# A transformer layer on one core: the last batch's shared up products moved from the late stage to the output stage

## The reference

```
x = x + cross_attention(layernorm(x), ctx)
xt = layernorm(x).reshape(2048, 512)
ids, probs = top 2 of (xt @ Wr + br + gate_bias), softmax over the two
routed:  u = xt @ Wup[e] + bup[e];  g = silu(u @ Wgate[e] + bgate[e]) * u;  eo = g @ Wdown[e] + bdown[e]
shared:  su = xt @ Wsu + bsu;  sg = silu(su @ Wsg + bsg) * su;  so = sg @ Wsd + bsd
out = x + sum over e of probs[e] * eo[e] + so
```

## Time and profile before

| | us |
|---|---|
| median of 3 runs | 1020.87 |
| lowest and highest run | 1019.53, 1021.21 |
| the profiled execution | 1023.9 |
| its span, first to last instruction | 1022.3 |
| PE busy in it | 927.3 |
| VectorE busy in it | 659.0 |
| GpSimd busy in it | 620.0 |
| ScalarE busy in it | 464.1 |
| output stage | from about 439 to 570.7 |
| routed stage | from 570.7 to 956.0 |
| late stage | from 956.0 to 1022.3 |

### The profile page before, as it was taken

How to read it: one execution, slowest core, us unless ns; L and a number is a source line. 1 busy time by engine, 2 the same in 40 slices (tenths; PEclk the granted TensorE clock), 3 DMA queues, 4 the chain that set the end, 5 groups by cost and what they waited for, 6 DMA issues and landing times. The chain is left out here.

```text
span 1022.3 us, 17154 instructions
## 1 busy us (share of the span) xinstructions
PE 927.3 (91%) x5077; PEld 406.1 (40%) x5078; DVE 659.0 (64%) x1026; ACT 464.1 (45%) x846; POOL 620.0 (61%) x565
## 2 busy tenths in 40 slices
PE   3799885799989999989999599999999999999998
PEld 1354542122212222246644244444544554554443
DVE  7787776688878788357765155554555555444388
ACT  3365565688878787522451022322322322322440
POOL 5465446377777674443047489898999999000373
PEclk9899998699999999989999699999999999999999
DMA  8135436345445432134427655555565664435566
GB/s 277 32 108 145 133 112 176 99 168 174 161 170 183 143 99 65 40 125 135 175 104 278 205 165 175 176 192 163 199 183 170 201 187 162 123 114 188 217 197 234
DMA packets 104521, 162.31 MB, mean 159 GB/s; under 512 B 10904, under 2 KB 53912, under 8 KB 104080
## 3 DMA queue, kind: packets, MB, share of 16 engines
q1 hardware_dynamic: 91520, 116.45, 35.1%
q0 software_dynamic: 12896, 45.10, 13.2%
q10 hardware_dynamic: 48, 0.05, 0.0%
HBM read 108.08 MB, written 53.48 MB: 158 GB/s over the span
## 5 line engine op out<-in xcount | busy, mean ns | idle before, releaser
L1060 DVE TENSOR_REDUCE nm<-quad 128x4 bf16<-128x1984 f32 x62 | 138.3, 2231 | 37.3 <-PE quad L1121 37.3
L1013 ACT ACTIVATE p_t<-a_psT 128x512 f32<-128x512 f32 x256 | 138.9, 595 | 48.0 <-PE a_psT L1136 46.6
L963 POOL TENSOR_TENSOR p_sum<-p_t,p_t 128x512 f32<-128x512 f32 x64 | 81.0, 1274 | 56.0 <-ACT p_t L1013 55.7
L1907 PE MATMUL quad<-w_exp,e_xT 128*128 x456 | 107.4, 387 | 7.3 <-issue 3.4
L1907 PE MATMUL e_psY<-w_exp,e_gT 128*128 x456 | 110.7, 380 | 0.9 <-ACT e_y L1848 0.9
L1907 PE MATMUL quad<-w_exp,e_uT 128*128 x456 | 106.6, 385 | 2.5 <-DVE e_uT L1862 2.5
L1136 PE MATMUL a_psT<-q_stk,k_stk 98*128 98x512 f16 x256 | 84.6, 401 | 12.1 <-ACT p_t L1013 9.4
L210 POOL TENSOR_TENSOR w_exp<-e_raw,w_exp 128x1024 f32 (+1 forms) x42 | 90.1, 2145 | 6.0 <-POOL e_raw L207 4.5
L202 POOL TENSOR_TENSOR w_exp<-e_raw,ws_tile 128x1024 f32 (+1 forms) x42 | 80.2, 1910 | 5.6 <-DMA e_raw<-in_L_ffn_Wup_dram 4.7
L1834 ACT ACTIVATE e_gT<-e_psGT 128x512 f16<-128x512 f32 x38 | 22.7, 597 | 124.7 <-PE e_psGT L1897 124.7
L1889 DVE TENSOR_TENSOR e_g<-e_g,e_u 128x512 f32<-128x512 f32 x38 | 58.6, 1542 | 26.4 <-ACT e_g L1855 26.4
(11 more groups left out here) (333 smaller groups left out, 1859.6 us busy)
## 6 DMA issues: line engine op xcount, KB each, us to landing
xs_dram<-zero SPq DMA_DIRECT2D x38, 256.0 KB, 7.2
e_x<-xs_dram SPq DMA_DIRECT2D x38, 256.0 KB, 4.1
bias<-in_L_ffn_bup_dram SPq DMA_DIRECT2D x38, 256.0 KB, 3.7
bias<-in_L_ffn_bgate_dram SPq DMA_DIRECT2D x38, 256.0 KB, 3.7
ys_dram<-e_y SPq DMA_DIRECT2D x38, 256.0 KB, 3.8
q_dram<-q_st SPq DMA_DIRECT2D x24, 256.0 KB, 3.0
k_dram<-k_st SPq DMA_DIRECT2D x24, 256.0 KB, 3.7
q_stk<-q_dram SPq DMA_DIRECT2D x64, 96.0 KB
```

What stands on the lines that cost most here:

```text
L963: pool.tensor_tensor(p_sum[:, w % SUMS, :], probs(w, 0), probs(w, 1), ALU.add).then_inc(s["sum_1"], 1)
L1013: act.activation(probs(w, k), psT[:, k % 2], ACT.Exp, scale=SCALE / (QS * QS)).then_inc(s["exp"], 1)
L1060: dve.tensor_reduce(nm[:, i, :, 0:1].rearrange("p h o -> p (h o)"), psS[:, :, 0:NMAIN], AX.X, ALU.max, negate=True)
L1907: ins = pe.matmul(dst[:, :], stationary, moving, start=(k == 0 and chunks[0] == 0), stop=(k == len(terms) - 1 and chunks[-1] == KD - 1))
```

## The change

- **Output stage.** PE makes the four up chunks of the last batch (grp 2, batch B - 1) after gate(1, ..) and before down(0, ..). ScalarE and VectorE make u and uT from them, in the buffers of group 0, and SyncE writes them in quarters to u_dram and uT_dram. Only batch 2 is still stored to xT_dram.
- **First routed rows.** SyncE waits for all scatters ahead of the store of tile 5 (m == TB + 1) and then loads the rows of blocks 0 and 1 into x_rows, a buffer that both stages share. The routed stage has no loads of its own for these two blocks.
- **Waits on the stores of y.** They leave SyncE's end of the output stage. ScalarE and VectorE wait for them ahead of the first step of the routed stage, and SyncE ahead of the load of of_first.
- **Late stage.** The up products of group 1 are gone. SyncE loads uT and u of group 1 first, ahead of the x1 tiles; gate(1, ..) waits for uT on PE and gated(1, ..) for u on VectorE. turned_probs(0) moves ahead of up(0, 3) on ScalarE. VectorE's gathered(m) are spread anew.
- **Gathers.** Eight transfers in flight (GATHERED) instead of four.

The diff, cut to this:

```diff
+GATHERED = 8
 ...
-    ORDER = (("u", 0), ("u", 1), ("g", 0), ("g", 1), ("d", 0), ("d", 1))
+    ORDER = (("u", 0), ("u", 1), ("g", 0), ("g", 1), ("u", 2), ("d", 0), ("d", 1))
+    BATCH = (0, 1, B - 1)
 ...
-            for b in range(B // 2, B):
-                sp.wait_ge(s["xT_l"], TB * (b + 1))
-                sp.dma_start(g_["xT_dram"][:, (b - B // 2) * KD * 2 * S:(b - B // 2 + 1) * KD * 2 * S],
-                             xT_all[:, b, :, :, :].rearrange("p k x s -> p (k x s)")).then_inc(xT_st[b - B // 2], 16)
+            sp.wait_ge(s["xT_l"], TB * (B // 2 + 1))
+            sp.dma_start(g_["xT_dram"], xT_all[:, B // 2, :, :, :].rearrange("p k x s -> p (k x s)")).then_inc(xT_st, 16)
+            for c in range(KD):
+                sp.wait_ge(s["u_l"], 2 * KD + c + 1)
+                sp.dma_start(g_["u_dram"][:, c * S:(c + 1) * S], u[2][:, c, :]).then_inc(g_["u_stored"], 16)
+                sp.dma_start(g_["uT_dram"][:, c * 2 * S:(c + 1) * 2 * S], uT[2][:, c, :, :].rearrange("p x s -> p (x s)")).then_inc(g_["u_stored"], 16)
             for m in range(NFIRST):
+                if m == TB + 1:
+                    for landed in scattered:
+                        sp.wait_ge(landed, 16 * TOP * NT // IN_FLIGHT)
+                    for n in range(2):
+                        sp.dma_start(first_rows[:, n], g_["xs_dram"][n * P:(n + 1) * P, :]).then_inc(x_rows_ld[n], 16)
                 sp.wait_ge(s["d_r"], m + 1)
 ...
-            for q in xT_st:
-                sp.wait_ge(q, 16)
-            for q in y_st:
-                sp.wait_ge(q, 8 * NFIRST)
+            sp.wait_ge(xT_st, 16)
 ...
+            for c in range(KD):
+                up(2, c)
 ...
+            for c in range(KD):
+                up_low(2, c)
             for j in range(TB):
                 down(0, j)
 ...
+            for c in range(KD):
+                up(2, c)
             for j in range(TB):
                 down(0, j)
 ...
-            load(0, 0)
             biases(0)
-            load(1, 1)
             run(sp, step)
 ...
+            for q in first_stored:
+                act.wait_ge(q, 8 * NFIRST)
             step(-1, 1, -1)
 ...
+            sp.dma_start(uT[:, 1].rearrange("p k x s -> p (k x s)"), g_["uT_dram"]).then_inc(uT_ld, 16)
+            sp.dma_start(u[:, 1].rearrange("p k s -> p (k s)"), g_["u_dram"]).then_inc(u_ld, 16)
 ...
-                if m >= IN_FLIGHT // TOP:
-                    before = m - IN_FLIGHT // TOP
+                if m >= GATHERED // TOP:
+                    before = m - GATHERED // TOP
 ...
+            turned_probs(0)
             up(0, 3)
-            turned_probs(0)
             turned_probs(1)
-            up(1, 0)
-            up(1, 1)
-            turned_probs(2)
-            turned_probs(3)
-            up(1, 2)
-            up(1, 3)
```

More of the change, by code:

```diff
@@ L1663, in up @@
                 free("u", grp, c)
-                pe.wait_ge(s["xT_l"], TB * grp + TB)
+                pe.wait_ge(s["xT_l"], TB * (BATCH[grp] + 1))
                 at = slice(c * P, (c + 1) * P)
-                product(chunk_bank("u", grp, c), [(weight(0, y, q)[:, at], xT_all[:, grp, q, x, :]) for q in range(KD)
+                product(chunk_bank("u", grp, c), [(weight(0, y, q)[:, at], xT_all[:, BATCH[grp], q, x, :]) for q in range(KD)
                                                   for x, y in ((0, 0), (1, 0), (0, 1))]).then_inc(s["u_mm"], 1)
@@ L1730, in routed @@
     y = sb(tag + "y", [P, 2, D], F32)
+    assert sb.at == SBUF_LO + E * g_["PER_E"] + 20480
+    sb.at += 2 * D * 4
     raw = sb("e_raw", [P, 2, 2, D], F32)
@@ L1889, in step @@
                     dve.tensor_tensor(g[:, :], g[:, :], u[:, j], ALU.mult).then_inc(s["g_r"], 1)
+            for q in first_stored:
+                dve.wait_ge(q, 8 * NFIRST)
             step(-1, 1, -1)
@@ L2094, in _ @@
                     gate(grp, c)
+                    if grp == 0 and c < 2:
+                        turned_probs(2 + c)
                     if c:
@@ L2141, in _ @@
             for c in range(KD):
-                up_low(1, c)
-                gathered(c)
-            for c in range(KD):
                 gated(0, c)
@@ L2147, in _ @@
                     gated_low(0, c - 1)
-                gathered(TB + c)
+                gathered(c)
             gated_low(0, KD - 1)
+            dve.wait_ge(u_ld, 16)
             for c in range(KD):
@@ L2154, in _ @@
                 first_total(c)
+                if c % 2:
+                    gathered(TB + c // 2)
             gated_low(1, KD - 1)
+            for m in range(TB + TB // 2, NFIRST):
+                gathered(m)
             for j in range(TB):
@@ L2183, in up @@
                 at = slice(c * P, (c + 1) * P)
-                product(chunk_bank("u", grp, c), [(weight(0, y, q)[:, at], xT[:, grp, q, x, :]) for q in range(KD)
+                product(chunk_bank("u", grp, c), [(weight(0, y, q)[:, at], xT[:, q, x, :]) for q in range(KD)
                                                   for x, y in ((0, 0), (1, 0), (0, 1))]).then_inc(s["u_mm"], 1)
@@ L2215, in _ @@
             pe.wait_ge(g_["split_done"], (E + 1) * (2 * NM) + 2 * NM + 1)
-            for c in range(UP_EARLY, KD):
-                up(0, c)
+            assert UP_EARLY == 2
+            up(0, 2)
             turn_probs(0)
+            up(0, 3)
             turn_probs(1)
-            up(1, 0)
-            up(1, 1)
-            turn_probs(2)
-            turn_probs(3)
-            up(1, 2)
-            up(1, 3)
             for c in range(KD):
                 gate(0, c)
-                if c >= 2:
+                if c < 2:
+                    turn_probs(2 + c)
+                else:
                     first_bias(c - 2)
```

42 lines of the change are left out of this document (29 added, 13 removed).

## The result

The changed kernel takes 1032.24 us (median of four runs, 1030.03 to 1034.18), the kernel before 1021.04 beside it: a ratio of 1.0117, 95% interval 1.0097 to 1.0138. It is slower, as forecast, but by 11.2 us where 3.5 were forecast, and 4 us above the upper end of the range. The profiled execution took 1034.18 us, its span is 1032.5. On every chip some executions of any kernel are slower at random; the medians and ratios of this document leave them out.

The account below looks back on a forecast made before the run. PE, 91% busy, was taken to bound the kernel, with VectorE the bound in the late stage. Terms 3.7 - 1.3 - 0.9 + 1.7 + 0.3 = +3.5 us on the median 1020.87 gave 1024.4, range 1021.2 to 1028.2.

Parts of the forecast that it names:

- The barrier: End of output stage: opens at 576.7 instead of 570.7, +6.0 us; first routed product at 579.8, +3.7.
- part 2: First rows loaded early, y-store waits moved: holds up nobody at tile 5's store; first routed product +3.7 us.
- The clock at the routed head: First routed products: clock falls as behind an earlier 4.09 us PE gap, perhaps for shorter; -1.3 us, between 0 and -4.1.
- Rival (a): Routed head and late stage: clock holds or is soon back at both; +0.6 us, 1021.5; chance 0.20.
- The late stage: Late stage: VectorE's account -0.9, half clock after PE's gap +1.7, small bd_raw loads +0.3; +1.1 us in all.
- The PE gap: Late stage, ahead of gate(0,0): PE idles 5.4 us waiting for uT, where it had no gap.
- +0.3: Late stage: small bd_raw loads delayed by 2.1 MB queued ahead of them; +0.3 us, range 0 to +5.4.
- rival (c): Late stage: small loads wait behind the added bytes; +8.6 us, 1029.5, or half of it, 1027; chance 0.09.
- PE is held instead: Late stage: first_bias(6) waits for first_total(4) behind 4.7 us of gathered pairs; expected wait 3 to 4 us.
- (b): Late stage: VectorE does not bind, moved pairs fit into its waits; -3.2 us, 1017.7; chance 0.07.
- (d): Routed stage: GpSimd's weights bind, so the barrier's +6.0 goes through whole; +7.1 us, 1028.0; chance 0.06.
- Eight gathers: 0: Late stage: eight gathers in flight cost 0, since VectorE's waits there name no gather.

Follow-up runs that it names:

- y_eight_buffers: Changed kernel with eight buffers for y instead of two, so VectorE's down sums wait for no store: 1028.4 us, ratio 1.0056 on chip 2.
- vector_order: Changed kernel with VectorE's late-stage list reordered (two gathered pairs ahead of the gates, first_total(4) and (5) earlier): 1029.2 us, ratio 1.0066 on chip 2.
- rows_alone: Kernel before with only the early load of the first routed rows and the moved y-store waits: 1018.5 us, ratio 0.9965 on chip 2.
- before_copy: Kernel before, unaltered, run again with a trace on chip 3: 1043.0 us, ratio 0.9991.
- after_third: Changed kernel, unaltered, run again beside the kernel before on chip 3: 1075.3 us, ratio 1.0307.
- four_again: Changed kernel with four gathers in flight instead of eight, on chip 3: 1051.3 us, ratio 1.0080.

## Why the prediction was right and wrong

**The barrier** was forecast 6.0 us later, the first product 3.7. Measured, with the 2.3 us taken off by which the stage started late: 8.4 (581.4 against the 570.7 of the earlier trace rows) and 6.0 (584.47 against 576.10). The first step that failed is "if that follows PE at once it ends at 576.0, if the stores pace it as now at 576.8. I take 576.2". Less those 2.3 the last sum ended at 578.3. I carried the pace of the stores over from the earlier trace rows (a store's landing took a median of 4.2 us) and said of the added SyncE traffic that it costs nothing, because the scatters meet the same traffic. The y stores do not: TensorE now runs without a gap to 577.5, eight y stores and eight stores of u and uT share the queue, and the longest of the y stores took 6.5. y_eight_buffers puts the mis-sized term at 1.6 to 2.3 us; how much of it the added stores make is not shown. Some 0.5 us of it comes from part 2, of which I wrote that it holds up nobody: SyncE issues the loads of x_rows (574.58) ahead of the store of tile 5 (575.43). From the last sum to the copy and from there to the product: forecast 2.0 and 1.6, measured 2.2 and 1.7. The number is right, in part by luck, since the transposes at the lower clock ended no earlier than the store landed.

**The clock at the routed head** was forecast at -1.3, on the row of the 4.09 gap. It fell again (5.30), and was back one block earlier: from the first transposes to the second product 11.15 us against 10.87, but that product in 2.76 instead of 4.45. Up to the product behind it that is -1.4, where -1.3 was forecast. But the same kernel on chip 4 has that second product slow too, and gains nothing there against the trace before:

```profile
590.87 4.45 PE L1937 MATMUL quad<-w_exp,e_uT 128*128 x12 [1.06 <-DVE e_uT L1890]
```

So the fall was forecast rightly, and the size was luck. Rival (a), the clock that holds, is out.

**The late stage** was forecast at +1.1 (-0.9, +1.7, +0.3) and came to +3.7. The PE gap: 5.4 forecast, 6.2 measured; half clock behind it: yes; the hold at first_bias(6): "3 to 4 us", 3.9 measured; no wait for a gather: right. bd_raw was used 8.73 us after the stage's start (971.30) instead of 7.87, so the +0.3 was 0.9, and rival (c) is out. What failed is the step between: "PE is held instead", after which the sum names no price. I took VectorE's account as the bound and let TensorE's holes vanish behind it. Without the hold, in vector_order, VectorE bounds the stage at 68.3, +2.1 (forecast 1.1); with it TensorE's chain comes to 70.0. So 1.6 of the missing 2.6 us are the hold with the clock it costs. The changed kernel's own trace says much the same: without its waits for TensorE at the end, 2.4 us in all, VectorE would have ended the stage at about 67.5 (an estimate).

TensorE's chain adds up from its rows. The 48 matmuls that are gone are -10.4, the gap +6.2, gate(0,0) at the lower clock +2.2 (979.69 - 974.94 = 4.75 instead of 2.59), the hold +3.9, and the lower clock behind it +1.6 (1014.88 - 1010.30 = 4.58 where 1003.23 - 1000.20 = 3.03 is usual): +3.5 of the 3.7 measured. With my own terms that chain would have been -10.4 + 5.4 + 2.5 + 3.5 = +1.0, no more than VectorE's +1.1. What it lacked above all is the clock that falls once more behind the hold (1.6), then 0.8 of the gap. Rows were at hand for it: the earlier trace rows has TensorE at 41.47 busy of 42.60, even fuller than VectorE. In the windows after (length; busy PE, PEld, DVE, ACT, POOL; granted clock; DMA share, GB/s) both are at 90%:

```profile
981.00:1025.00 44.00, 39.81 (x178) 17.59 (x177) 39.56 (x59) 9.71 (x17) 19.46 (x18) 0.96 0.70 241
```

With two engines so even, a hole in either has to be priced in its own chain, with the clock behind it, and the larger sum taken.

**Rivals (b) and (d).** VectorE was not free (late stage longer, not shorter), and no wait for GpSimd's weights longer than in the earlier trace rows appeared (the routed stage is 381.0).

**The rest.** Stages account for +7.9 us (5.9 - 1.7 + 3.7), the medians differ by 11.2, on chip 4 by 9.5. The trace before is not typical: its routed stage took 382.7 where rows_alone has 379.4, and its late stage 66.2 where the same code has 67.1 in rows_alone. Against rows_alone the differences of these stages would be +1.6 and +2.8, and the sum 10.3. So the rest lies within the scatter of single stages, and no run assigns it to the change. That -1.7 in the routed stage looks like my -1.1 is chance.

**Eight gathers: 0** was right for the chip of the forecast and for chip 4, and wrong by 24 us and more elsewhere, which nothing in the trace before shows.

## What to carry to other kernels

Where two engines are both near full in a stage, write down each one's own chain with its holes and the half-clock stretch behind each hole, and take the later: a wait that "moves to the other engine" has a price until its chain is shown to end earlier. Added work that is free for TensorE and VectorE may still be paid in buffers: if a sum waits for the store of two sums before, a slower store goes into the path, and here more buffers took it out again. And take the halves of a change apart: here the small one alone gained 0.35% on one chip, while the whole lost about 1%.

## What the runs showed of the hardware

The kernel before took 1021 to 1022 us in the first pair and on chips 2 and 4, and 1041 to 1045 on the three others, and nearly all of the difference lies in one place: from the first gate chunk of the output stage to the first transpose 71.2 us instead of 50.0, while GpSimd issues 32 scatters. TensorE in before_copy goes one matmul at a time there, some 20 us after the first scatter, and goes on without gaps 4 us after the last (the POOL row):

```profile
551.82 0.58 PE L1659 MATMUL quad<-f_uT,w_exp 128*128 128x512 f16 x1 [1.48 <-issue]
553.21 0.59 PE L1659 MATMUL quad<-f_uT,w_exp 128*128 128x512 f16 x1 [0.81 <-issue]
...
561.47 0.96 POOL L1382 DMA_INDIRECT xs_dram<-xn,slot  x1 [0.30 <-issue]
...
566.60 5.46 PE L1659 MATMUL quad<-w_exp,f_gT 128*128 128x512 f16 x18 [0.84 <-issue]
```

The late stage of after_third is the same picture in large. VectorE, GpSimd and TensorE:

```profile
1012.88 0.75 DVE L2136 TENSOR_TENSOR l_g<-l_g,l_u 128x512 f32<-128x512 f32 x1 [17.31 <-issue]
...
1015.40 0.95 POOL L2079 DMA_INDIRECT l_yr<-ys_dram,slot  x1 [0.31 <-issue]
...
1021.19 0.61 PE L2247 MATMUL l_psP<-bd,pT 128*128 128x512 f16 x1 [22.28 <-ACT pT L2108]
```

and its windows, in the columns above:

```profile
995.00:1005.00 10.00, 3.91 (x21) 1.73 (x18) 0.57 (x1) 0.00 (x0) 7.57 (x9) 0.91 1.03 381
1005.00:1015.00 10.00, 0.00 (x0) 0.00 (x0) 0.75 (x1) 0.69 (x1) 7.57 (x9) 0.50 0.74 216
```

Nearly everything but GpSimd is at a standstill until GpSimd's last gather (1015.40); 5 us later all run. In four_again, on the same chip, GpSimd has to wait for landings and there is no standstill:

```profile
1002.00:1012.00 10.00, 10.00 (x50) 4.75 (x49) 8.32 (x13) 5.26 (x9) 7.86 (x8) 1.00 0.72 215
...
1018.18 0.95 POOL L2079 DMA_INDIRECT l_yr<-ys_dram,slot  x1 [1.29 <-DMA l_yr<-ys_dram,slot]
```

What the rows have in common: on those chips an unbroken train of indirect DMAs, one in 1.26 us for over 20 us, brings an engine stall that sets in some 20 us after the train's start and outlasts it by 4 to 5 us. On the other chips the same trains run without one: in the changed kernel's first trace 32 gathers in 41.2 us. It is not a full DMA: the share was 0.50 in 520 to 560 of before_copy. The Trainium skill (Runtime: NRT & Kernel Launch, "Instruction fetch mechanics") says that each engine refills its small instruction memory over a DMA queue of its own; held engines that wait for nothing but issue would fit that, and no packet of the instruction queues shows between 995 and 1016 in after_third. But on chip 4, where nothing stalls, 980 to 1000 shows none either. The cause stays open, as does what differs between the chips. For use: four gathers in flight, which cost nothing measurable on the other chips, take the late stage's stall away. The number alone is no cure: the scatters also run with four in flight, their landings keep up, so GpSimd waits for none and the stall of the output stage stays.
